# A two-layer transformer in fp32 on one core: new piece tables and TensorE's layer 0 rounds written out

## What is computed

```python
x = x + _layernorm(_L0_attn_ref(_layernorm(x), Wq, bq, Wk, bk, Wv, bv, Wo, bo))
x = x + _layernorm(_L0_ffn_ref(_layernorm(x), w_gate, w_up, w_down))
x = x + _layernorm(_L1_attn_ref(_layernorm(x), Wq, Wk, Wv, Wo))
x = x + _layernorm(_L1_ffn_ref(_layernorm(x), W_r, W_k, W_v, mu_r, mu_k))
```

## Time and profile before

| | before |
|---|---|
| runs (us) | 1496.42, 1495.2, 1499.88; median 1496.42 |
| profiled execution (us) | 1490.64 |
| its span (us) | 1488.8 |
| mean granted clock of TensorE | 0.994 |
| matmuls | 12438 |

### The profile page before, as it was taken

The page is one execution under the profiler, slowest core; times in us unless marked ns, Lnnn a source line. Parts: engine busy times, 40 slices in busy tenths (PEclk is TensorE's granted clock), DMA queues, the critical chain, the costliest instruction groups (busy, mean ns, idle before and its releaser), DMA issues. The chain is left out here.

```text
span 1488.8 us, 32925 instructions
## 1 busy us (share of the span) xinstructions
PE 1402.8 (94%) x12438; PEld 1042.0 (70%) x12438; DVE 1082.9 (73%) x2067; ACT 800.0 (54%) x1135; POOL 788.5 (53%) x994
## 2 busy tenths in 40 slices
PE   5889999999999998999999999999999999999996
PEld 4566767676767675777777777767677677677775
DVE  7888888888888877755567585585685665765766
ACT  2555444444444445555766656656556666566652
POOL 4344434444444442444666575666575565766652
PEclk8999999999999999999999999999999999999999
DMA  5221212112020122100100000010100100100001
GB/s 182 83 86 48 72 58 73 58 58 70 36 78 25 67 80 100 43 29 29 65 2 1 15 29 2 1 44 1 43 1 1 43 1 1 43 1 30 2 1 43
DMA packets 36547, 61.40 MB, mean 41 GB/s; under 512 B 3760, under 2 KB 19024, under 8 KB 36432
## 3 DMA queue, kind: packets, MB, share of 16 engines
q1 hardware_dynamic: 35568, 59.09, 11.4%
q10 hardware_dynamic: 864, 0.66, 0.2%
HBM read 25.86 MB, written 8.42 MB: 23 GB/s over the span
## 5 line engine op out<-in xcount | busy, mean ns | idle before, releaser
L1740 ACT ACTIVATE l_probs<-psum 128x1024 f32<-128x1024 f32 (+1 forms) x192 | 164.5, 879 | 165.2 <-PE psum L2074 127.8
L929 ACT ACTIVATE l_probs<-psum 128x512 f32<-128x512 f32 x256 | 138.3, 593 | 175.2 <-PE psum L1195 165.8
L321 POOL TENSOR_SCALAR_AFFINE_SELECT l_probs<-l_probs 128x256 f32<-128x256 f32 (+1 forms) x384 | 179.4, 498 | 0.0
L1012 DVE TENSOR_REDUCE l_rowmax<-psum 128x2 f32<-128x1024 f32 (+2 forms) x192 | 158.9, 862 | 20.4 <-PE psum L1156 19.8
L1836 DVE TENSOR_TENSOR l_qk_lo<-psum,l_qk_hi 128x1024 fp32r<-128x1024 f32 x64 | 77.6, 1218 | 117.0 <-ACT l_qk_hi L1730 116.5
L2117 PE MATMUL psum<-l_probs,l_v 128*32 128x512 f32 (+3 forms) x2048 | 151.8, 434 | 11.6 <-DVE l_qk_lo L1836 9.8
L1746 ACT ACTIVATE l_probs<-l_probs 128x2048 f32<-128x2048 f32 (+1 forms) x128 | 160.4, 1274 | 1.3
L1845 DVE RECIPROCAL l_keysum<-psum 128x256 f32<-128x256 f32 x64 | 112.3, 1754 | 44.0 <-PE psum L2103 37.4
L2117 PEld LDWEIGHTS psum<-l_probs,l_v 128*32 128x32 f32 x2048 | 65.5, 110 | 92.8 <-issue 80.2
L316 POOL TENSOR_TENSOR l_pool_holder<-expo 128x1 f32<-128x1 f32 x128 | 26.2, 204 | 195.5 <-ACT l_probs L1746 130.0
L1858 DVE TENSOR_TENSOR l_att<-psum,l_keysum 64x256 f32<-64x256 f32 x256 | 107.8, 421 | 15.9 <-PE psum L2117 9.1
(11 more groups left out here) (240 smaller groups left out, 4134.8 us busy)
## 6 DMA issues: line engine op xcount, KB each, us to landing
...
```

The source lines that it names most:

```text
L321: nc.gpsimd.affine_select(out=part, in_=part, compare_op=ALU.is_ge, fill=0.0, base=0, pattern=[[0, part.shape[1]], [1, P]], channel_multip ...
L929: space.free(nc.scalar.activation(probs[:, SLOT[p], e, c0:c1], space.unit(*use), ACT.Exp, scale=HD0 ** -0.5), *use)
L1012: reduced = nc.vector.tensor_reduce(rowmax[:, a // 2, :, a % 2, t], space.unit("max", a, k)[:, :, c0:c0 + (t + 1) * P], mybir.AxisListType ...
L1740: space.free(nc.scalar.activation(probs[:, p % 2, :, c0:c1], space.unit("score", p, u)[:, :, 0:c1 - c0], ACT.Tanh, scale=HD1 ** -0.5 / CLA ...
```

## The change

It gives new places to nearly all pieces in both layers (inside and outside the loops), to the loads of the weights and to the end rounds, and new banks to most uses in layer 0; in layer 1 only qk(1) and the heats at the very end get others. The pieces stay the same, with the same instructions; the number of heats too. The one line of code that changes has PE's program of layer 0 written out for rounds 3 to 6, as layer 1's is. The tables cut to what the text speaks of:

```diff
@@ -543,138 +543,138 @@ phase1: table
-        "heat": {(0,): 41.175, (1,): 40.388, (2,): 17.176, (3,): 38.128, (4,): 40.332, (5,): 40.403},
+        "heat": {(0,): 39.441, (1,): 36.863, (2,): 39.44, (3,): 36.273, (4,): 39.437, (5,): 39.526},
...
-        "tail": {(0,): 16.059, (1,): 18.367, (2,): 25.801, (3,): 28.021},
+        "tail": {(0,): 15.446, (1,): 18.567, (2,): 26.216, (3,): 29.302},
...
-        "maxima": {(0,): 16.769, (1,): 19.946, (2,): 38.478, (3,): 40.111},
+        "maxima": {(0,): 14.777, (1,): 18.462, (2,): 23.268, (3,): 32.762},
...
@@ -682,29 +682,29 @@ phase1: program, bank_table
         play(sorted(once + schedule.before(), key=lambda entry: entry[0]), pieces)
-        schedule.loop(eng, pieces)
+        schedule.loop(eng, pieces, unrolled=eng.engine == nc.tensor.engine)
         tail_pieces[eng.engine] = pieces
...
-        "heat": {(0,): 7, (1,): 2, (2,): 7, (3,): 2, (4,): 2, (5,): 3},
+        "heat": {(0,): 6, (1,): 7, (2,): 4, (3,): 3, (4,): 6, (5,): 4},
...
-        "tail": {(0, 0): 2, (0, 1): 6, (1, 0): 5, (1, 1): 4, (2, 0): 5, (2, 1): 0, (3, 0): 7, (3, 1): 4},
+        "tail": {(0, 0): 2, (0, 1): 3, (1, 0): 4, (1, 1): 5, (2, 0): 1, (2, 1): 0, (3, 0): 5, (3, 1): 4},
...
@@ -1369,67 +1369,67 @@ phase2: table
-        "recip": {(0,): 3.48, (1,): 7.76, (2,): 15.07, (3,): 15.13, (4,): 16.56, (5,): 21.83, (6,): 26.797, (7,): 26.93},
+        "recip": {(0,): 8.195, (1,): 12.57, (2,): 13.463, (3,): 15.722, (4,): 15.729, (5,): 24.244, (6,): 27.442, (7,): 28.1},
...
-        "qk_lo": {(0,): 1.878, (1,): 2.109, (2,): 3.32, (3,): 3.408, (4,): 10.596, (5,): 15.055, (6,): 15.131, (7,): 17.208},
+        "qk_lo": {(0,): 2.342, (1,): 2.54, (2,): 4.221, (3,): 4.328, (4,): 12.582, (5,): 14.049, (6,): 15.142, (7,): 21.073},
...
-        "x4_rstd": {(): 52.383},
+        "x4_rstd": {(): 48.712},
-        "x4_rstd": {(0,): 280.645, (5,): 428.145, (6,): 558.094, (7,): 586.933},
+        "x4_rstd": {(0,): 272.238, (5,): 445.508, (6,): 544.246, (7,): 583.133},
...
-        "x4_norm": {(): 51.224},
+        "x4_norm": {(): 52.099},
-        "x4_norm": {(0,): 296.15, (5,): 429.983, (6,): 534.707, (7,): 592.658},
+        "x4_norm": {(0,): 299.497, (5,): 454.965, (6,): 529.323, (7,): 592.44},
...
@@ -1524,16 +1524,16 @@ phase2: load table
-        "load": {(0,): 203.592, (1,): 170.206, (2,): 193.357, (3,): 170.207, (4,): 263.379, (5,): 261.668, (6,): 281.294, (7,): 279.261, (8,): 298.223, (9,): 289.222},
+        "load": {(0,): 207.906, (1,): 209.887, (2,): 209.112, (3,): 184.872, (4,): 217.484, (5,): 216.238, (6,): 279.702, (7,): 285.768, (8,): 288.712, (9,): 291.156},
```

More of the change, by code:

```diff
@@ L545, in phase1 @@
     table = {
[L546 to L562, removed]
@@ L565, in phase1 @@
[L565 to L568, removed]
@@ L577, in phase1 @@
[L577 to L594, removed]
@@ L604, in phase1 @@
-        "tail": {(0,): 16.059, (1,): 18.367, (2,): 25.801, (3,): 28.021},
-        "exp_tail": {(0,): 15.534, (1,): 19.256, (2,): 25.598, (3,): 32.182},
+        "load_x": {(): -15.319},
+        "x_stats": {(): -18.194},
+        "x_rstd": {(): -22.344},
+        "x_norm": {(): -17.22},
+        "x_T": {(0,): -13.659, (1,): -12.596},
+        "x_T_hi": {(0,): -9.127, (1,): -9.12},
+        "x_T_lo": {(0,): -12.303, (1,): -12.14},
+        "rope": {(0,): -7.674, (1,): -4.98, (2,): 0.001, (3,): 4},
@@ new lines, in phase1 @@
+        "roped": {(0,): -8.605, (1,): -6.14, (2,): -0.179, (3,): 4.411},
+        "turned": {(0,): -6.156, (1,): -1.94, (2,): 1.536, (3,): 4.779},
+        "rope_sum": {(0,): -8.306, (1,): -2.88, (2,): -0.549, (3,): 1.2},
+        "rope_hi": {(0,): 0.714, (1,): 1.819, (2,): 10.747, (3,): 11.088},
+        "rope_lo": {(0,): -5.469, (1,): -2.077, (2,): 1.716, (3,): 2.001},
+        "place": {(0,): 1.911, (1,): 8.633, (2,): 18.456, (3,): 15.926},
+        "v": {(0,): 9.867, (1,): 10.245},
+        "v_out": {(0,): 14.138, (1,): 14.813},
@@ new lines, in phase1 @@
+        "o_stats": {(): 37.091},
+        "o_rstd": {(): 36.857},
+        "residual": {(): 42.459},
+        "o_norm": {(): 37.818},
+        "x1_stats": {(): 38.26},
+        "x1_rstd": {(): 39.429},
+        "x1_norm": {(): 39.636},
+        "gate": {(0,): 44.145, (1,): 44.8, (2,): 48.256, (3,): 49.306, (4,): 50.214, (5,): 51.733},
+        "tanh": {(0,): 44.75, (1,): 49.549, (2,): 52.277, (3,): 52.616, (4,): 55.616, (5,): 56.388},
+        "gated": {(0,): 41.858, (1,): 44.211, (2,): 48.237, (3,): 49.537, (4,): 50.909, (5,): 52.507},
@@ L669, in phase1 @@
+        "residual": {(0,): -20.577, (1,): 68.869, (6,): 184.732, (7,): 235.814},
+        "store": {(0,): 68.782, (5,): 184.554, (6,): 222.194, (7,): 289.306},
     }
@@ new lines, in phase2 @@
+        "x3_T": {(0,): 279.39, (1,): 310.027, (6,): 502.111, (7,): 581.175},
+        "key": {(0,): 282.928, (1,): 314.582, (6,): 519.054, (7,): 588.538},
+        "r": {(0,): 283.415, (1,): 315.069, (6,): 520.936, (7,): 594.353},
+        "out": {(0,): 286.229, (1,): 317.504, (6,): 543.988, (7,): 596.235},
+        "end_heat": {(0, 7): 596.259, (1, 7): 572.79, (2, 7): 596.297, (3, 7): 578.987, (4, 7): 596.336, (5, 7): 585.038, (6, 7): 580.562, (7, 7): 580.726, (8, 7): 583.304},
+        "x3_T_b": {(7,): 583.058},
@@ L1503, in phase2 @@
+        "load_x": {(0,): 210.853, (1,): 226.082, (2,): 291.091, (3,): 292.463},
+        "residual": {(0,): 291.028, (1,): 305.775, (2,): 320.671, (7,): 502.811},
+        "store": {(0,): 292.489, (1,): 312.376, (6,): 469.571, (7,): 521.743},
+        "store_b": {(7,): 547.83},
     }
```

397 lines of the change are left out of this document (201 added, 196 removed), and 9 rows, old and new, of the table moved_table.

## The result

The changed kernel takes 1457.38 us (median of 4 runs, 1455.56 to 1462.04) against 1495.81 (4 runs of the kernel before beside them, 1491.91 to 1499.88): a ratio of 0.9748, 95% interval 0.9712 to 0.9783, or 38 us. 20 us were forecast, and the range ended at 1461 on the low side, 3.6 us above the result. The sign and the places were right, the size was half. The profiled execution took 1455.56 us, its span is 1453.8, 35.0 us shorter than before.

What follows compares the result with a forecast made beforehand. PE (TensorE) was taken to bound the kernel, busy 1402.8 of 1488.8 us, leaving 86 idle. The terms -4 + 0 - 9 - 5 - 2 = -20 us, off the median 1496.42, gave 1476.5 us, range 1461 to 1500.

Steps and rivals of the forecast that it cites:

- Layer 1: Four middle rounds of layer 1: PE's two waits for qk_lo go, smaller new waits come, -2.3 us a round, -9 in all.
- the queue at qk(2): Layer 1 middle round: qk(2) waits for the bank of recip(7) and att(7), now queued behind x4_norm, 0.9 us taken.
- Layer 0: Four middle rounds of layer 0: waits for banks and a row maximum go, smaller ones come, -1.0 us a round, -4.
- The banks of the heats: Layer 0 middle round: new banks for heat 0 and heat 4 end two 0.7 us waits for exponentials, removing 1.4 us.
- The wait at pv(0): Layer 0 middle round: fewer matmuls cover exponential and masks before pv(0), some 1.2 us of wait where 0.6 was.
- max(3,0)'s 1.2: Layer 0 middle round: the 1.2 us wait for a row maximum goes, since its new bank has a whole score before it.
- D: Rival, whole kernel: more is gained, the bounds on the good side, about -33 us, 1463 us; chance 0.06.
- Between the loops: Stretch between the two loops: the 4.8 us wait for maxima and 2.5 of half clock go, 2 left for shuffled waits, -5.
- The start: Kernel start: earlier roped and turned shorten waits by 1.7 and 2 to 3 us, lost matmul cover costs 2.1, net -2.
- A: Rival, layer 1: x4_norm stays at 6.7 us beside POOL work, layer 1 gives +4, 1489.4 us; chance 0.16.
- B: Rival, both layers and between the loops: every removed wait comes back at the next claim, 1496 us; chance 0.13.
- C: Rival, layer 1: a new wait of about 4 us at qk(2) drops PE's clock, +20 in four rounds, 1505 us; chance 0.11.

## Why the prediction was half of it

By medians, moving x4_rstd and recip(3) alone brought 18.8 of the 38.4 us and SP's order 2.8. If these add up, the other 17 come from the rest of the new tables, and no run takes those apart. By the prediction's own steps:

- **Layer 1, -9 forecast, -20 measured: the step that failed.** It is 11 of the 15 us by which the profiled execution went beyond the forecast. The causes were right: late x4_rstd and qk_lo(6) behind recip(3), 3.5 us forecast, 3.7 measured by putting in those two alone. What was charged against them was too much: 0.9 for the queue at qk(2) (8.8 - 8.0 of its own terms is 0.8), measured 0.5, and 0.3 at x3_T, where no wait shows. And what was left standing was the larger error: I kept the five small waits, 1.5 us a round, and they went down to 0.2, and PE's busy time fell by 0.86 a round, which my sum had fixed with the number of matmuls. By difference 5.0 - 3.7 + 0.5 = 1.8 us a round came from the rest of the new order, 7 us in four. The whole lists of DVE and POOL were reordered, and I had followed the moves that touched the two largest waits. Which of the other moves brought the 1.8 is not separated and stays open.
- **Layer 0, -4 forecast, -9.5 measured.** My sum of parts was wrong on both sides. The banks of the heats, -1.4 in it, are worth nothing by themselves in the old order. The wait at pv(0), +0.6 in it, didn't come: from tail(0)'s end to pv(0) are 4.3 us now, not 3.5, and the masks take 1.36 and 1.35 where the first took 1.96. max(3,0)'s 1.2 behaved as said. I took -1.0 a round; it was -2.1 in the round shown and -2.4 on the average of four. Which of the many moves brought the rest was not separated and stays open.
- **The bounds were no bounds.** "All waits named go with nothing new" would have been -2.6 a round by the sum for layer 0 (-10), not -2.0 (-8), and -3.5 for layer 1 (-14), not -2.8 (-11). And the good bounds as they stand add up to -8 - 1 - 11 - 9 - 8 = -37, where D says -33. With the named waits in full the lower end would have been -42, at 1454; the measured 1457.4 lies above that. For layer 1 alone even -14 is short of -20.
- **Written-out rounds, 0 forecast:** no effect was measured, but up to 3.7 us of gain is not excluded.
- **Between the loops, -5 forecast:** idle fell by 4.1: the wait for the maxima went from 4.8 to 0.4, the rest of the idle time from 6.0 to 6.3, and the slow clock behind that wait is gone. SP's order alone shortens the stretch by 3.6 where I had taken 7.3 out, so a fall near -5 is in part luck. By how much the whole change shortened the stretch can't be told, since matmuls moved into it.
- **The start, -2 forecast:** the chain is shorter as said, max(0,0) starts at 27.51 instead of 28.90, but the stretch's idle fell by 0.4 only. The waits for turned (5.6 us) are gone; in their place PE idles 8.9 us ahead of max(0,0), for the DMA of the rotated q, and the clock is 0.53 and 0.61 from 20 to 40 us, where it was 0.79 and 0.70. Together with the stretch between the loops -7 was forecast, and -5.5 measured.
- **The base.** The sum was made against a profiled execution without one slow-clock round and then taken off the median. The medians differ by 38.4, the profiled executions by 35.1; rounds like those of 104 us are one thing that sets the two apart.
- **Rivals.** A (x4_norm stays at 6.7): no, 3.1. B (waits change places): true of heats' banks, not of the rest. C (half clock in layer 1 from a wait of 4 us, and none under it): its mechanism exists, but in the kernel *before*, already behind 2.4 us, and the change took it away. The rival to the other side was drawn from the wrong kernel. D was the nearest, at 1463 with 6%.
